# A transformer block on one core: another front, an earlier key-and-value split, a reordered expert stage

## The reference

```python
mod = silu(c) @ w_mod                      # per batch: sa, ca, ga, sb, cb, gb
h = layernorm(x) * (1 + ca) + sa
q, k, v = relu(h Wq), relu(h Wk), h Wv     # 16 heads of 32
vk = sum over tokens of [v, 1] k^T         # per batch and head
o = (vk q)[:-1] / (vk q)[-1]
x = x + clamp(ga) * (o Wproj + b)
h = layernorm(x) * (1 + cb) + sb
x = x + clamp(gb) * (top-2-of-8 experts of h + shared expert of h)
```

## Time and profile before

| | |
|---|---|
| median of 3 runs | 1218.13 us (1217.94 to 1220.59) |
| profiled execution, device time | 1217.89 us |
| its span (first to last instruction) | 1216.1 us |
| mean granted TensorE clock | 0.996 of full |
| PE busy | 1189.8 us, 98% |
| DVE busy | 805.9 us, 66% |
| ACT busy | 417.7 us, 34% |
| POOL busy | 506.3 us, 42% |
| share of PE in the chain that ended last | 90% |

### The profile page before, as it was taken

The page is one execution under the profiler, slowest core; times in us unless marked ns, Lnnn a source line. Parts: engine busy times, 40 slices in busy tenths (PEclk is TensorE's granted clock), DMA queues, the critical chain, the costliest instruction groups (busy, mean ns, idle before and its releaser), DMA issues.

```text
span 1216.1 us, 25326 instructions
## 1 busy us (share of the span) xinstructions
PE 1189.8 (98%) x9054; PEld 776.8 (64%) x9054; DVE 805.9 (66%) x1578; ACT 417.7 (34%) x873; POOL 506.3 (42%) x409
## 2 busy tenths in 40 slices
PE   7999999999999999999999999999999999999996
PEld 2646666666666666767777777656666666666663
DVE  5647778878776777655857754266666666666665
ACT  4424444445443432333323323222222222222221
POOL 2212566656564554222112112345445554455543
PEclk9999999999999999999999999999999999999998
DMA  7816597998788978745434535579787897779783
GB/s 238 228 40 168 125 250 192 214 234 212 182 222 185 229 209 197 173 99 120 122 87 104 137 85 117 111 150 135 132 141 140 131 132 139 138 135 136 133 127 45
DMA packets 253255, 185.27 MB, mean 152 GB/s; under 512 B 186496, under 2 KB 198784, under 8 KB 253132
## 3 DMA queue, kind: packets, MB, share of 16 engines
q1 hardware_dynamic: 217368, 114.40, 42.1%
q0 software_dynamic: 20512, 45.62, 22.4%
q10 hardware_dynamic: 15256, 23.62, 6.7%
HBM read 87.07 MB, written 52.75 MB: 115 GB/s over the span
## 4 chain that ended last, share of the span: by engine, by line
PE 90%; DVE 2%; issue 2%; DMA 2%; POOL 1%; ACT 1%; SPq 0%; ACTq 0%; POOLq 0%; DVEq 0%
PE ps_o L87 7%; PE ps_o L89 7%; PE ps_o L88 7%; PE ps_vs L87 6%; PE ps_vs L88 6%; PE ps_vs L89 6%; PE ps_kh L87 4%; PE ps_vh L87 4%; PE ps_vh L88 4%; PE ps_vh L89 4%; PE ps_kh L88 4%; PE ps_kh L89 4%; PE ps_qh L87 4%; PE ps_qh L89 4%; PE ps_qh L88 4%
## 5 line engine op out<-in xcount | busy, mean ns | idle before, releaser
L444 POOL DMA_INDIRECT out<-y,slot_row x71 | 139.3, 1963 | 190.3 <-DVE y L882 138.7
L89 PE MATMUL ps_o<-w_all,xt 128*128 x568 | 177.5, 313 | 0.0
L88 PE MATMUL ps_o<-w_all,xt 128*128 x568 | 177.5, 313 | 0.0
L87 PE MATMUL ps_o<-w_all,xt 128*128 x568 | 177.5, 312 | 0.0
L874 DVE SCALAR_TENSOR_TENSOR gate_row<-gate_rows,batch_weight,gate_row 128x512 f32<-128x512 f32 x213 | 158.9, 746 | 2.5
L368 POOL DMA_INDIRECT out<-s_sum,row_no x32 | 53.8, 1680 | 197.6 <-DVE s_sum L623 192.0
L1133 ACT ACTIVATE at<-ps_y 128x384 f16<-128x384 f32 x71 | 34.8, 491 | 250.7 <-PE ps_y L1353 247.1
L330 POOL TENSOR_TENSOR h<-cen,rows_f 128x512 f32<-128x512 f32 x32 | 40.6, 1270 | 130.6 <-ACT cen L901 115.4
L89 PE MATMUL ps_qh<-ht,wqkv 128*128 128x128 f16 x512 | 87.4, 219 | 0.0
L88 PE MATMUL ps_qh<-ht,wqkv 128*128 128x128 f16 x512 | 87.4, 219 | 0.0
L87 PE MATMUL ps_qh<-ht,wqkv 128*128 128x128 f16 x512 | 87.4, 219 | 0.0
(11 more groups left out here) (251 smaller groups left out, 3341.2 us busy)
## 6 DMA issues: line engine op xcount, KB each, us to landing
w_stage<-in_w_d ACTq DMA_DIRECT2D x64, 176.0 KB
xb<-in_x SPq DMA_DIRECT2D x32, 256.0 KB, 3.7
xr<-in_x SPq DMA_DIRECT2D x32, 256.0 KB, 4.0
out<-x SPq DMA_DIRECT2D x32, 256.0 KB, 3.6
h_d<-hl SPq DMA_DIRECT2D x32, 256.0 KB, 2.5
h2t_d<-h2t SPq DMA_DIRECT2D x32, 256.0 KB, 3.5
s_ht<-h2t_d SPq DMA_DIRECT2D x32, 256.0 KB, 3.6
sstage<-in_sh_flat SPq DMA_DIRECT2D x32, 136.0 KB, 3.6
```

Source lines behind the costliest of these rows:

```text
L87: nc.tensor.matmul(out, lh, rh, start=first, stop=False, skip_group_check=True)
L88: nc.tensor.matmul(out, lh, rl, start=False, stop=False, skip_group_check=True)
L89: return nc.tensor.matmul(out, ll, rh, start=False, stop=last, skip_group_check=True)
L444: pool.indirect_dma_start(m.out, bass.IndirectOffsetOnAxis(ap=m.slot_row[:, t:t + 1], axis=0), m.y[:, t % Y_RING, :], None, compute_op=ALU ...
```

## The change

1. **Front.** The conditioning row is computed once for all four batches: `sct_rep` holds each batch's column 32 times. It is copied to `modrows`, and PE spreads batch 0's row over the partitions by a product with ones (two matmuls). `modulate(0)` and `(1)` are gone. PE runs matmuls on ones before the weights arrive (11) and in two later places (3 each). Tile 0 is normalised on DVE alone, turned by four transposes on PE, and split out of PSUM in halves (`turned_high`, `turned_low`); its transposing DMA, its POOL `shift` and its ACT `scale` are gone. The waits of the first tile's projections are cut up by weight piece.
2. **Weights at the front.** All `stage` pieces are issued by SP (ring of 8, was 6), two of them between the `wmod` pieces. The low parts of pieces 5 and 6 go to POOL, behind a scaling on ACT.
3. **Later conditioning weights.** Their eight loads and two small ones move from ACT's queue to SP's, at steps 0 and 1, ahead of the step's transposing DMA.
4. **Shared pieces.** Load and split of the 32 `sh` pieces start at step 2; steps 16 and 17 take two each.
5. **Border.** `vk_low` of the last batch stands straight behind `divide` of step 32.
6. **Experts.** The two `at` buffers lie apart, so `e_high(0)` no longer waits for the shared expert's last sum and is ahead of ACT's first gate row; DVE's multiply of tile 1 is ahead of the gate rows. The last `e_turn` stands within the last but one `e_down`, and the last tile's first gate row and low part ahead of that tile's predecessor's output.

```diff
@@ sync_program
     for k in range(KC):
         sp.dma_start(m.wmod[:, k, 0:2 * C], ...).then_inc(m.wmod_loaded[k], 16)
-    for n in range(KC):
+        if 1 <= k < 3:
+            sp.dma_start(m.stage[:, k - 1, :], m.pieces[k - 1][0]).then_inc(m.stage_loaded[k - 1], 16)
+    load_x(1)
+    for n in range(2, 2 * KC):
         sp.dma_start(m.stage[:, n, :], m.pieces[n][0]).then_inc(m.stage_loaded[n], 16)
-    load_x(1)
     load_x(2)
+    for n in range(2 * KC, 3 * KC):
+        sp.wait_ge(m.stage_lo, n - STAGE_RING + 1)
+        sp.dma_start(m.stage[:, n % STAGE_RING, :], m.pieces[n][0]).then_inc(m.stage_loaded[n % STAGE_RING], 16)
...
+        if 0 <= s <= 1:
+            sp.wait_ge(m.bc_done, 2)
+            for k in range(KC):
+                cols = slice((2 + 2 * s) * C, (4 + 2 * s) * C)
+                sp.dma_start(m.wmod[:, k, cols], ...).then_inc(m.wmod_loaded[s], 16)
...
         turn_h(s + 2)
@@ gpsimd_program
+        if s == -1:
+            split_low(POOL_SPLITS[0])
         shift(s + 2)
+        if s == -1:
+            split_low(POOL_SPLITS[1])
@@ vector_program, ahead of the loop
+    stats(0)
+    v.wait_ge(m.rstd_done, 1)
+    v.tensor_scalar(m.cen[:, 0, :], m.xb[:, 0, :], m.mv[:, 0, 0:1], m.rstd[:, 0, :], ALU.subtract, ALU.mult).then_inc(m.cen_done, 1)
+    split_low(0)
+    split_low(1)
+    v.wait_ge(m.bc_done, 1)
+    v.tensor_scalar(m.modrows[:, C:2 * C], m.ps_o[:, 1, :], 1.0, None, ALU.add).then_inc(m.row_done, 1)
+    stats(1)
+    v.wait_ge(m.spread_done, 1)
+    v.tensor_tensor(m.h[:, 0, :], m.cen[:, 0, :], m.ps_row[CA], ALU.mult).then_inc(m.scaled, 1)
+    v.wait_ge(m.spread_done, 2)
+    v.wait_ge(m.scaled, 1)
+    v.tensor_tensor(m.h[:, 0, :], m.h[:, 0, :], m.ps_row[SA], ALU.add).then_inc(m.h_done, 1)
+    centre(1)
+    turned_low(0)
+    turned_low(1)
+    for n in (2, 3, 4, 7):
+        split_low(n)
+    h_low(1)
+    for n in (8, 9):
+        split_low(n)
+    k_low(0)
+    for n in (10, 11):
+        split_low(n)
+    v_low(0)
+    stats(2)
+    for s in range(TILES + TAIL):
...
             divide(t)
+            if s == TILES:
+                vk_low(B - 1)
             low(q - 1)
...
-        if 0 < s <= TILES and s % BT == 0:
+        if 0 < s < TILES and s % BT == 0:
             vk_low(s // BT - 1)
@@ scalar_program, ahead of the loop
+    for n in range(3):
+        split_high(n)
+    act.wait_ge(m.bc_done, 2)
+    act.activation(m.modrows[:, 0:C], m.ps_o[:, 0, :], ACT.Copy).then_inc(m.row_done, 1)
+    for n in range(3, 6):
+        split_high(n)
+    scale_stage(POOL_SPLITS[0])
+    act.wait_ge(m.h_done, 1)
+    act.activation(m.rows_f[:, 0, SA, :], m.ps_row[SA], ACT.Copy).then_inc(m.row0_done, 1)
+    turned_high(0)
+    turned_high(1)
+    scale(1)
+    split_high(6)
+    scale_stage(POOL_SPLITS[1])
+    split_high(7)
+    h_high(1)
+    split_high(8)
+    split_high(9)
+    k_high(0)
...
+    v_high(0)
@@ tensor_program, ahead of the loop
+    pe.wait_ge(m.consts, ONE_READY)
+    keep_busy(WARM)
     pe.wait_ge(m.rep_done, KC)
     for k in range(KC):
         pe.wait_ge(m.wmod_loaded[k], 16)
-        for r in (0, 1):
+        for r in (CA, SA):
             mm = nc.tensor.matmul(m.ps_o[:, r, :], m.sct_rep[:, k, :], m.wmod[:, k, r * C:(r + 1) * C], ...)
...
-    modulate(0)
-    pe.wait_ge(m.row0_done, 2)
-    modulate(1)
+    pe.wait_ge(m.row_done, 2)
+    for r in (CA, SA):
+        nc.tensor.matmul(m.ps_row[r], m.one[0:1, :], m.modrows[0:1, r * C:(r + 1) * C], start=True, stop=True).then_inc(m.spread_done, 1)
+    keep_busy(FILL)
+    pe.wait_ge(m.h_done, 1)
+    for k in range(KC):
+        mm = nc.tensor.transpose(m.ps_first[k // 2][:, k % 2, :], m.h[:, 0, k * P:(k + 1) * P], m.ident[:, :])
+        if k % 2:
+            mm.then_inc(m.first_turned, 1)
+    keep_busy(FILL)
@@ e_down
         for k in range(IT):
+            if turn_within and k == 1:
+                e_turn(t + 1)
```

More of the change, by code:

```diff
@@ L157, in turn_h @@
     def turn_h(i):
-        if tile(i):
+        if tile(i) and i >= PE_TURNED:
             sp.wait_ge(m.h_lo, i + 1)
@@ L369, in add_shared @@
                                     compute_op=ALU.add).then_inc(m.shared_added[u], 16)
+    step(pool.memset(m.one[:, :], 1.0))
     step(pool.memset(m.minus_half[:, :], -0.5))
+    step(pool.memset(m.ident[:, :], 0.0))
+    step(pool.affine_select(out=m.ident[:, :], in_=m.ident[:, :], compare_op=ALU.not_equal, fill=1.0,
+                            base=0, pattern=[[-1, P]], channel_multiplier=1))
     step(pool.memset(m.v_sb[:, :, 0, :, P:P + 1], SCALE))
@@ L682, in vector_program @@
         h2_low(t - 2)
-        for n in SPLITS_LAST.get(s, ()):
-            split_low(n)
-        v_low(s)
-        if s == 0:
-            v.wait_ge(m.mod_done, 2)
-            v.tensor_scalar(m.mod[:, C:2 * C], m.ps_o[0:B, 0, :], 1.0, None, ALU.add).then_inc(m.mod_copied, 1)
+        if s > 0:
+            v_low(s)
         if s < TILES:
@@ L886, in vector_program @@
     for t in range(1, SLOT_TILES + 1):
-        e_low(t - 1)
-        gate_rows_of(t - 1, 1)
+        last = t == SLOT_TILES - 1
+        if t < SLOT_TILES:
+            e_low(t - 1)
+        if t == 1:
+            e_multiply(t)
+        if t < SLOT_TILES:
+            gate_rows_of(t - 1, 1)
         gate_rows_of(t - 1, 2)
-        if t < SLOT_TILES:
+        if last:
+            gate_rows_of(t - 1, 3)
+        if 1 < t < SLOT_TILES:
             e_multiply(t)
-        gate_rows_of(t - 1, 3)
+        if last:
+            gate_rows_of(t, 1)
+            e_low(t)
+        else:
+            gate_rows_of(t - 1, 3)
         e_out(t - 1)
@@ L977, in split_high, with scale_stage @@
         act.activation(m.pieces[n][1][:, 0, :], m.stage[:, n % STAGE_RING, :], ACT.Copy, scale=SCALE).then_inc(m.stage_hi, 1)
+    def scale_stage(n):
+        act.wait_ge(m.stage_hi, n + 1)
+        act.activation(m.stage[:, n % STAGE_RING, :], m.stage[:, n % STAGE_RING, :], ACT.Copy, scale=SCALE).then_inc(m.stage_scaled, 1)
     def activate(q):
@@ L1273, in down, with keep_busy @@
             nc.tensor.matmul(out, m.s_at[:, j, 0, tok], m.sh[:, 1, lo:lo + C], start=False, stop=True, skip_group_check=True).then_inc(m.sy_done, 1)
+    def keep_busy(count):
+        for _ in range(count):
+            nc.tensor.matmul(m.ps_y[:, 0:P], m.one[:, :], m.one[:, :], start=True, stop=True)
+    pe.wait_ge(m.consts, ONE_READY)
+    keep_busy(WARM)
     pe.wait_ge(m.rep_done, KC)
@@ L1354, in e_turn, with e_down @@
         mm.then_inc(m.at_done, 1)
-    def e_down(t, expert):
+    def e_down(t, expert, turn_within=False):
         pe.wait_ge(m.e_at_lo, t + 1)
@@ L1378, in tensor_program @@
             pe.wait_ge(m.s_t1_done, 2 * CHUNKS)
-        e_down(t - 1, expert)
+        e_down(t - 1, expert, t == SLOT_TILES - 1)
         expert = following
-    e_turn(SLOT_TILES - 1)
     e_down(SLOT_TILES - 1, expert)
```

224 lines of the change are left out of this document (117 added, 107 removed).

## The result

| | median us | runs | span of the profiled run |
|---|---|---|---|
| before | 1218.13 | 1216.93 to 1220.59 (5) | 1216.1 |
| changed | 1210.50 | 1210.11 to 1211.32 (5) | 1209.6 |

The ratio is 0.9937, 95% interval 0.9924 to 0.9950: 7.6 us faster. 1207.7 was predicted; the result lies inside the range, 2.8 us above the forecast and between the forecast and rival 1 (1211.2). The profiled execution is the slowest of its five, so its span shows 6.5 us of gain.

A forecast was written before the change was run, and what follows sets the result against it. PE, busy 1189.8 of 1216.1 us, was taken to bound the kernel. Gains of 7.1 + 1.4 + 1.6 + 0.3 = 10.4 us gave 1207.7 us on the median, range 1205.0 to 1211.8.

The forecast's parts named there:

- rival 1: Front: DVE and POOL collide more, or the clock falls; 3.5 us more in all, 1211.2 us; chance 0.18.
- Front: Start of kernel to step 2: step 2 starts at about 37.1 instead of 44.21, 7.1 us gained, bounds 5.5 to 8.0.
- Step 0: First attention step: bound by DVE, done at 26.0 with 1.0 us of POOL contention; step 1 starts at 28.3.
- SP's queue: Steps 0 and 1: 2 MB of loads ahead of each transposing DMA cost nothing, 1.6 us to spare each.
- Rival 3: SP's queue at steps 0 and 1: transposing DMAs wait behind slow loads, about 1219 us and up; chance 0.03.
- Border: Step 32 on: attend(24) starts 2.1 us earlier, 0.7 given back at tile 24's output; 1.4 us, bounds 0 to 2.1.
- Experts: Start of the experts: PE's wait ahead of e_down(0) goes; 1.6 us gained, bounds 1.2 to 1.6.
- End: Last e_down: the 1.26 us wait on transposes becomes one for e_out(69); 0.3 us gained, bounds 0 to 0.6.
- Rival 2: Border and experts: edits bring nothing, PE's gain given back to DVE's chain; 1210.0 us; chance 0.13.
- rival 4: Front and border: DVE is quicker than forecast, front gives 8.5 and border 2.1 us; 1205.6 us; chance 0.12.
- The signs: First projection about 18, step 2 at 37, full clock between, DVE never idle 18 to 26, attend(24) released by logits.
- signs of being wrong: First projection after 21, a PE wait on ht at step 2 or 3, or steps 33 to 35 waits over 2 us.

The follow-up runs named there:

- e1: Changed kernel with vk_low of the last batch back at the end of step 32; 1212.31 us, ratio 0.9954.
- e3: Changed kernel with five more matmuls on ones between the conditioning rows and the wait for their copies; 1210.52 us.
- e7: Changed kernel with statistics and centring of tile 2 ahead of v_low(0) on DVE; 1211.31 us.
- e8: Changed kernel with the sh pieces split one per step from step 0, as before the change; 1212.14 us, ratio 0.9954.
- e11: Changed kernel with division ahead of product from step 32, conditioning-row gap filled, and spread by a 128x128 matrix; 1207.56 us, ratio 0.9922.
- e5: Changed kernel with all low halves of the first weight pieces on DVE, none on POOL; 1211.44 us, ratio 0.9944.
- e2: Kernel before with only the early vk_low at step 32; 1217.76 us, ratio 1.0003.
- e12: Kernel before with the division ahead of the shared experts' product from step 32 on, vk_low still late; 1213.33 us, ratio 0.9967.
- e9: Changed kernel with the start of the experts as before: first gate row ahead of e_high(0), tile 1's multiply behind the gate rows; 1214.87 us, ratio 0.9979.
- e6: Changed kernel with the division ahead of the shared experts' product on DVE in every step from 32 on; 1206.95 us, ratio 0.9906.

## Why the prediction came out as it did

The mechanisms were the ones named and no engine or queue stopped the change. The size was 2.8 us too large, nearly all of it in the front. In the profile the four terms give 3.93 (front, at step 31), 0.90, 1.79 and 0.10 us, 6.7 in sum, where 7.1, 1.4, 1.6 and 0.3 were predicted.

*Front, 7.1 predicted.* 4.66 at step 2 in the changed kernel, 4.54 to 5.08 in e1 and e3 to e7, 2.98 to 4.08 in e8 to e11. All of this is below the lower bound of 5.5 that the prediction gave; the time is inside its range only because the range reached down to rival 1 as a whole. This is the term that was mis-sized, in three parts, shown in e1's figures, whose clock did not fall: 

- The first key projection is at 18.53, not 17.9. The conditioning rows end at 13.56, predicted 13.0, and the spread starts at 14.34, predicted 13.8. Where the clock falls, 0.7 to 1.6 come on top.
- Step 0 takes 11.17 us, not 10.4. "Beside them POOL has `shift(1)` and the split of piece 6 ... I count 1.0": it was 2.0, shown by four splits in 4.53 and borne out by e5. The 1.0 came from a misread row. The split of 1.08 us lost 0.45, and the prediction set this against all 1.26 us of POOL's `shift`; but the split started at 19.09 and the shift ended at 19.62, so 0.45 was lost in 0.53 us. A second pair in the kernel before says the same, 0.71 lost in 0.80 us:

```profile
23.58 1.34 DVE L591 SCALAR_TENSOR_TENSOR wqkv<-stage,wqkv 128x512 f16<-128x512 f32 x1 [0.30 <-ACT wqkv L977]
```

```profile
23.11 1.27 POOL L330 TENSOR_TENSOR h<-cen,rows_f 128x512 f32<-128x512 f32 x1 [2.52 <-ACT cen L901]
```

At these rates 2.5 us of POOL's work would have cost 2.1 to 2.2, near what was measured. The Trainium skill (GPSIMD Engine Reference, Specifications) has the SBUF interfaces of GpSimd shared with VectorE, with contention for instructions with two SBUF inputs. The trace agrees in kind: DVE lost 2.0 us beside 3.09 of POOL's, neither the 1.0 nor the full 2.5 of the prediction.
- Step 1 takes 9.58 us, not 8.8. From the end of `v_low(0)` to that of `v_low(1)` 10.3 us were predicted, and it takes 11.08 in the changed kernel (27.65 to 38.73). 0.67 of the 0.8 us lie ahead of the end of `h_low(2)` (33.32), and of these 0.40 are POOL's power, which was left out; the rest is spread over the statistics and the hand-overs. PE waits 0.87 for `v_low(1)`. The one other order on DVE that was tried (e7) doesn't buy this back.

0.6, 0.8 and 0.8 make the 2.2 us between 7.1 and e1's 4.93. A further 0.4 to 0.7 went between step 2 and step 31 in six of the eleven profiles with the changed front, 0.72 in the changed kernel's own; why is open.

*SP's queue, no cost predicted.* Right for the changed kernel: the first set of loads is issued from 26.1, `ht(2)` at 33.35, and PE never waits for `ht`. Rival 3 is out. But the 1.6 us to spare weren't there: PE waits for `ht(3)` in e3 (0.18 us) and in e7 (0.56).

*Border, 1.4 predicted.* `attend(24)` was free 1.97 us earlier, 2.1 predicted, and what held it then was the copy of the logits (399.53 to 399.69 on ACT), as said. Given back: 1.54 us, 0.7 predicted. The transposing DMA was issued as predicted: 411.79 less 407.32 is 4.47, of which 3.93 are the loop's, so 0.54 from the border (0.6 predicted). It took 5.0 us to PE's start, where 3.9 had been assumed. A further 0.47 us came behind `project_out(24)`, 0.39 of it in e1 too, so it isn't the border's; one wait for `s_at` fell from 0.76 (583.96) to 0.33 (579.13). It is 0.31 to 0.33 in every other profile, also in e2 and e12, so the 0.76 may be a matter of that one execution. With the early split the gain from step 31 to the experts is 0.90 to 1.75 in the eight profiles with the product first, 0.33 without it (e1): 0.6 to 1.4 us.

*Experts, 1.6 predicted.* 1.79 us by the positions; but undoing it (e9) costs 4.4 in time, the clock's part included. The prediction priced the wait that it saw. It did not ask how late the load that ends it can land.

*End, 0.3 predicted.* 0.1: the new wait of 0.98 us for `e_out(69)` stands where 1.26 stood.

*Rival 1* had both its halves in part: more contention, and a clock that fell. It took the fall for something that follows a long gap; here it came 1.5 to 2.5 us after the end of a wait of 0.78 us, with PE busy in between. The Trainium skill (TensorE: Matmul & The Clock Gate, Part 1) has the low level as the default and activity as what releases it; by that the filled front would have stayed at the full level, and four of the eleven profiles with the changed front show 0.50. The result, 1210.50, lies nearer to rival 1's 1211.2 than to the forecast. *Rival 2* was half right by its argument (given back to the chain), *rival 4* wrong. Against rival 2 the prediction said that DVE was never over 1.1 us idle in a step there. At the head of step 32 the trace of before has DVE idle for 1.81 us (the row in e12), and this is the idle time that e6 and e12 turned into time won.

*The signs.* `attend(24)` waited 0.55 us for the logits, and DVE had no idle time from 18.2 to 26, as named. The first projection (19.19 for 18), step 2 (39.55 for 37) and the clock (0.50 for full) were missed. One of the signs of being wrong did show: the waits in steps 33 and 34 sum to 2.22 us (0.55 and 1.67), over the 2 us named.

One more reading was unsound: from 10.11 us for 16 conditioning matmuls it was concluded that half ran at the low clock. They now take 7.31, so the gain was real, but the granted clock reads 1.00 from 6 to 11 us in both kernels; what made them slow isn't shown:

```profile
6.00:11.00 5.00, 5.00 (x6) 2.03 (x7) 0.00 (x0) 0.15 (x1) 0.00 (x0) 1.00 1.03 406
```

This is the kernel before; the row of the changed kernel stands above, with twelve records in the same 5 us.

## What to carry to other kernels

In an in-order queue look for an operation that waits at the head while ready work stands behind it: swapping one product and one division was worth 4.2 us here on an engine that was 66% busy, and with it more of the gain at the border stayed. When a wait is removed ahead of a load or DMA, price the next one by its own time from issue to use, and not by the wait seen now. Before work is moved to POOL, look in the trace at what DVE's operations lose beside POOL's, over the time in which the two overlap: here it was two thirds or more, and two splits worth 1.2 us of DVE's time bought 0.24 when moved.

## What the hardware showed that wasn't expected

The granted clock can fall while PE is busy: from 17 to 20 us at 0.50 in the changed kernel with PE busy all the time, after a wait of only 0.78 us at 13.5; in the kernel before, 2.51 us without a matmul at the border left it at 1.00. Of profiles with the same front up to there some show it and some don't. The same holds for the wait ahead of the first key projection in the kernels with the old front: 2.45 us (before) and 2.01 us (e2) were followed by 0.50, 2.16 us in e12 were not. And 3.99 us without a matmul in e9 were followed by 0.50. The load of the gate rows takes 6.8 to 10.2 us from issue to use for the same bytes, the transposing DMA of tile 24's output 4.2 to 5.6 us to PE's start.
